# Two routing stages of a four-block graph and mixture kernel: sums, tables, semaphores and bias loads rearranged

## The reference, cut to what matters

```python
top_vals, top_idx = jax.lax.top_k(logits, K)          # K = 2, 8 or 16 experts
w = jax.nn.softmax(top_vals, axis=-1)
h = act(x @ W1[e] + b1[e])                            # gelu in the first, relu in the second
y = y + (h @ W2[e] + b2[e]) * w[..., e]               # only for the two chosen experts
```

## Time and profile before

| | us |
|---|---|
| median of 3 runs | 1710.01 (1708.18 to 1711.74) |
| the profiled execution, whole | 1711.71 |
| its span, first to last instruction | 1709.0 |
| PE busy | 1495.1 (87%) |
| DVE busy | 845.1 (49%) |
| ACT busy | 484.4 (28%) |
| POOL busy | 337.4 (20%) |

### The profile page before, as it was taken

The page is one execution under the profiler, slowest core; times in us unless marked ns, Lnnn a source line. Parts: engine busy times, 40 slices in busy tenths (PEclk is TensorE's granted clock), DMA queues, the critical chain, the costliest instruction groups (busy, mean ns, idle before and its releaser), DMA issues. The chain is left out here.

```text
span 1709.0 us, 33464 instructions
## 1 busy us (share of the span) xinstructions
PE 1495.1 (87%) x8648; PEld 1051.6 (62%) x8648; DVE 845.1 (49%) x2423; ACT 484.4 (28%) x1258; POOL 337.4 (20%) x391
## 2 busy tenths in 40 slices
PE   3796899999999999974999957897999829999976
PEld 3685654457444855544999942344666629899964
DVE  6897753333232467775222238411688652222227
ACT  2565310013000311111444433100233304445434
POOL 3000210013000300002455530000001224555530
PEclk9855899999999999985999979999999759999989
DMA  4000331124111422222223347402122245332436
GB/s 127 0 0 1 96 96 48 48 84 129 49 49 59 133 90 86 86 65 95 93 95 117 120 132 240 129 25 70 56 73 65 87 153 162 119 118 93 145 97 184
DMA packets 134635, 158.57 MB, mean 93 GB/s; under 512 B 16929, under 2 KB 119698, under 8 KB 134258
## 3 DMA queue, kind: packets, MB, share of 16 engines
q1 hardware_dynamic: 122642, 125.59, 23.4%
q0 software_dynamic: 11840, 32.12, 6.2%
q10 hardware_dynamic: 96, 0.20, 0.0%
HBM read 103.12 MB, written 57.93 MB: 94 GB/s over the span
## 5 line engine op out<-in xcount | busy, mean ns | idle before, releaser
L891 PE MATMUL layer_ps<-parts,counts 128*128 128x512 f16 x1875 | 409.1, 379 | 1.2 <-issue 0.6
L891 PEld LDWEIGHTS layer_ps<-parts,counts 128*128 (+1 forms) x1875 | 183.3, 98 | 217.7 <-issue 2.7
L1419 ACT ACTIVATE experts_hT<-experts_ps_h,experts_b_col 128x128 f32<-128x128 f32 x456 | 159.8, 367 | 102.8 <-PE experts_ps_h L1394 81.6
L1402 PE MATMUL experts_ps_y<-experts_rows,experts_hT 128*128 128x256 f32 x688 | 164.0, 381 | 1.1 <-ACT experts_hT L1419 0.2
L1357 POOL DMA_INDIRECT chosen<-experts_y,experts_row x116 | 114.6, 988 | 152.6 <-issue 130.0
L1402 PEld LDWEIGHTS experts_ps_y<-experts_rows,experts_hT 128*128 128x128 f32 x688 | 123.9, 190 | 16.7 <-ACT experts_hT L1419 3.2
L792 POOL TENSOR_TENSOR parts<-layer_rest,gru_rows 128x256 f32 (+2 forms) x75 | 54.5, 726 | 392.8 <-DVE layer_rest L767 392.8
L1346 POOL DMA_INDIRECT experts_fetched<-tokens,experts_index x120 | 116.1, 967 | 77.6 <-issue 45.1
L953 DVE COPY layer_total<-layer_ps 128x256 f32<-128x256 f32 x75 | 31.8, 425 | 183.5 <-PE layer_ps L891 180.6
L1394 PEld LDWEIGHTS experts_ps_h<-experts_xT,experts_rows 128*128 128x128 f32 x976 | 120.0, 194 | 4.0 <-DVE experts_xT L1435 0.9
L1394 PE MATMUL experts_ps_h<-experts_xT,experts_rows 128*128 128x128 f32 x976 | 120.4, 277 | 0.5 <-DVE experts_xT L1435 0.5
(11 more groups left out here) (315 smaller groups left out, 2080.1 us busy)
## 6 DMA issues: line engine op xcount, KB each, us to landing
experts_rows<-in_L_ffn_w SPq DMA_DIRECT2D x32, 512.0 KB, 5.0
gru_rows<-x SPq DMA_DIRECT2D x75, 128.0 KB, 2.1
own<-layer_own SPq DMA_DIRECT2D x75, 128.0 KB, 1.7
layer_own_in<-own SPq DMA_DIRECT2D x75, 128.0 KB, 2.1
h<-layer_out SPq DMA_DIRECT2D x50, 128.0 KB, 1.7
gru_rows<-h SPq DMA_DIRECT2D x50, 128.0 KB, 2.1
gru_rows<-chosen SPq DMA_DIRECT2D x50, 128.0 KB, 2.4
combine_y<-chosen SPq DMA_DIRECT2D x50, 128.0 KB, 2.4
```

The source lines that it names most:

```text
L891: last = nc.tensor.matmul(ps[b][:], cst.counts[:, s, bass.ds(t * P, P)], parts[:, s, :], start=s == 0, stop=s == NT - 1)
L1402: last = nc.tensor.matmul(ps_y[:, 0:D], hT[:, c, :], down[b][:, c, :], start=c == 0, stop=c == KH - 1)
L1419: nc.scalar.activation(hT[:, c, :], ps_h[c][:, 0:P], function, bias=b1_col[:, bass.ds(e * KH + c, 1)]).then_inc(hT_ready, 1)
```

## The change: what it does

1. `clear()` ahead of `route` is replaced by `hand_over()`, which only returns the list; POOL clears those semaphores inside `route`, after its constants. The barrier of L103 is gone there (it stays at the program's end).
2. DVE waits for `consts` ahead of its third instruction and no more ahead of its first.
3. `either` and `upto` are laid out [128, E, 25]. The running sum over tiles is made on DVE from `either`, ahead of the product with all ones. PE adds into one bank: (triangle minus ones) times `either`, then ones times `upto`. The product for the counts takes only the last tile's E columns. POOL makes the matrix `not_before`. The slot then takes one DVE instruction in place of three.
4. The tables of the second choice are made in two pieces, tiles 0 to 15 and 16 to 24, and PE starts on the first when it is there.
5. At the end two instructions (`second`, `free_row`) go behind the one that writes `plan.token`.
6. The output biases: for E = 16 they are loaded in `route`, behind the four experts' weights on SP. For E = 8 the load stays in `run_experts` but waits until the second gather has landed.

```diff
+    def hand_over(self):
+        old, self.held = self.held, []
+        return old
+
+    def clear_behind(self, old):
+        self.nc.clear_and_free_semaphores(old)
...
+        CUT = 2 * NT // 3
+        PIECES = ((slice(0, NT),), (slice(0, CUT), slice(CUT, NT)))
...
+                if expert_weights.b2_all is not None:
+                    sp.dma_start(expert_weights.b2_all[:], expert_weights.b2.partition_broadcast(P)).then_inc(
+                        expert_weights.b2_loaded, 16)
...
+                whole = lambda a: a[:].rearrange("p e t -> p (e t)")
+                pe.wait_ge(minus_ready, 1)
                 pe.wait_ge(picked, 1)
-                by_expert = either[:].rearrange("p t e -> p e t")
-                nc.tensor.matmul(ps_sum[:, 0:NT * E], cst.ones[:], by_expert, start=True, stop=True).then_inc(summed, 1)
-                nc.tensor.matmul(ps_rank[:, 0:NT * E], cst.before[:], by_expert, start=True, stop=True).then_inc(ranked, 1)
+                nc.tensor.matmul(ps_rank[:, 0:NT * E], not_before[:], whole(either), start=True, stop=False)
+                pe.wait_ge(running, 1)
+                nc.tensor.matmul(ps_sum[:, 0:E], cst.ones[:], upto[:, :, NT - 1], start=True, stop=True).then_inc(summed, 1)
+                nc.tensor.matmul(ps_rank[:, 0:NT * E], cst.ones[:], whole(upto), start=False, stop=True).then_inc(ranked, 1)
                 pe.wait_ge(bounds_ready, 1)
                 plan.ends_pe = tile_ends(nc, pe, plan, slice(0, E))
                 for c in range(2):
-                    pe.wait_ge(placed, c + 1)
-                    for t in range(NT):
-                        last = nc.tensor.matmul(ps_token[c][:, 0:MT], at_place[c][:, :, t], token_at[c][:, :, t],
-                                                start=t == 0, stop=t == NT - 1, skip_group_check=True)
+                    for i, piece in enumerate(PIECES[c]):
+                        pe.wait_ge(placed, c + i + 1)
+                        for t in range(piece.start, piece.stop):
+                            last = nc.tensor.matmul(ps_token[c][:, 0:MT], at_place[c][:, :, t], token_at[c][:, :, t],
+                                                    start=t == 0, stop=t == NT - 1, skip_group_check=True)
                     last.then_inc(tokens_known, 1)
...
-                dve.wait_ge(consts, 1)
...
+                    if c == 0:
+                        dve.wait_ge(consts, 1)
...
-                nc.vector.tensor_tensor(either[:], chosen[:, 0], chosen[:, 1], ALU.add).then_inc(picked, 1)
+                nc.vector.tensor_tensor(either[:].rearrange("p e t -> p t e"), chosen[:, 0], chosen[:, 1], ALU.add).then_inc(
+                    picked, 1)
+                dve.drain()
+                nc.vector.tensor_tensor_scan(upto[:].rearrange("p e t -> p (e t)"), first_of[:].rearrange("p e t -> p (e t)"),
+                                             either[:].rearrange("p e t -> p (e t)"), 0.0, ALU.mult, ALU.add).then_inc(
+                    running, 1)
...
                 dve.wait_ge(summed, 1)
-                nc.vector.tensor_tensor_scan(upto[:].rearrange("p e t -> p (e t)"), first_of[:].rearrange("p e t -> p (e t)"),
-                                             ps_sum[:, 0:NT * E], 0.0, ALU.mult, ALU.add)
...
-                nc.vector.tensor_scalar(tiles_i[:], upto[:, :, NT - 1], float(P - 1), None, ALU.add)
+
+                nc.vector.tensor_scalar(tiles_i[:], ps_sum[:, 0:E], float(P - 1), None, ALU.add)
...
-
-                nc.vector.tensor_tensor(upto[:].rearrange("p e t -> p (e t)"), upto[:].rearrange("p e t -> p (e t)"),
-                                        ps_sum[:, 0:NT * E], ALU.subtract)
-                dve.drain()
-                nc.vector.scalar_tensor_tensor(upto[:], base[:].unsqueeze(2).to_broadcast([P, E, NT]), float(P), upto[:],
+                dve.wait_ge(ranked, 1)
+                nc.vector.scalar_tensor_tensor(slot.rearrange("p t e -> p e t"), base[:].unsqueeze(2).to_broadcast([P, E, NT]),
+                                               float(P), ps_rank[:, 0:NT * E].rearrange("p (e t) -> p e t", t=NT),
                                                ALU.mult, ALU.add)
-                dve.wait_ge(ranked, 1)
-                dve.drain()
-                nc.vector.tensor_tensor(slot[:].rearrange("p t e -> p e t"),
-                                        ps_rank[:, 0:NT * E].rearrange("p (e t) -> p e t", t=NT), upto[:], ALU.add)
...
-                    nc.vector.tensor_tensor(at_place[c][:], number[:], to_all(slot_at[0][:, c], P), ALU.is_equal)
-                    if c > 0:
+                    for piece in PIECES[c]:
+                        to_all = lambda a, n: a[:, piece].unsqueeze(1).to_broadcast([P, n, piece.stop - piece.start])
+                        nc.vector.tensor_tensor(at_place[c][:, :, piece], number[:, :, piece], to_all(slot_at[0][:, c], P),
+                                                ALU.is_equal)
+                        if c > 0:
+                            dve.drain()
+                        nc.vector.tensor_tensor(token_at[c][:, :, piece], number[:, 0:MT, piece], to_all(slot_at[1][:, c], MT),
+                                                ALU.is_equal)
                         dve.drain()
-                    nc.vector.tensor_tensor(token_at[c], number[:, 0:MT, :], to_all(slot_at[1][:, c], MT), ALU.is_equal)
-                    dve.drain()
-                    nc.vector.tensor_tensor(token_at[c], token_at[c], to_all(token_code[:], MT), ALU.mult).then_inc(placed, 1)
+                        nc.vector.tensor_tensor(token_at[c][:, :, piece], token_at[c][:, :, piece], to_all(token_code[:], MT),
+                                                ALU.mult).then_inc(placed, 1)
...
+                dve.drain()
+                nc.vector.tensor_scalar(empty, code, 0.0, float(HALF), ALU.is_le, ALU.add)
+                dve.drain()
+                nc.vector.scalar_tensor_tensor(plan.token[:], code, -1.0, empty, ALU.add, ALU.add).then_inc(token_ready, 1)
                 nc.vector.tensor_scalar(second, ps_token[1][:, 0:MT], 0.0, float(NP), ALU.not_equal, ALU.mult)
-                dve.drain()
-                nc.vector.tensor_scalar(empty, code, 0.0, float(HALF), ALU.is_le, ALU.add)
                 nc.vector.tensor_scalar(free_row, code, 0.0, spare_row[:, 0:1], ALU.is_equal, ALU.mult)
                 dve.drain()
-                nc.vector.scalar_tensor_tensor(plan.token[:], code, -1.0, empty, ALU.add, ALU.add).then_inc(token_ready, 1)
...
                 nc.gpsimd.memset(first_of[:, :, 0:1], 0.0).then_inc(consts, 1)
+                nc.gpsimd.tensor_tensor(not_before[:], cst.before[:], cst.ones[:], ALU.subtract).then_inc(minus_ready, 1)
+                pool.drain()
                 iota(token_no[:], [[P, NT]], 1, -HALF)
                 iota(spare_row[:], [[0, 1]], 1, 2 * NP - HALF)
                 iota(number[:], [[1, P], [0, NT]], 0).then_inc(numbered, 1)
+                cst.semaphores.clear_behind(old)
...
-                sp.dma_start(b2_all[:], b2.partition_broadcast(P)).then_inc(b2_loaded, 16)
+                if b2_here:
+                    sp.wait_ge(fetch_done[1], 16)
+                    sp.dma_start(b2_all[:], weights.b2.partition_broadcast(P)).then_inc(b2_loaded, 16)
...
-                cst.semaphores.clear()
+                old = cst.semaphores.hand_over()
```

More of the change, by code:

```diff
@@ L1072, in tile_ends, with route @@
     return ends
-def route(nc, cst, dr, tag, E, logit, plan, expert_weights):
+def route(nc, cst, dr, tag, E, logit, plan, expert_weights, old):
     with ExitStack() as ctx:
@@ L1096, in route @@
         base = sb("base", [P, E])
-        slot = either
+        slot = either[:].rearrange("p e t -> p (e t)").rearrange("p (t e) -> p t e", e=E)
+        not_before = sb("not_before", [P, P])
         slot_f, slot_i = sb("slot_f", [P, 2, NT]), sb("slot_i", [P, 2, NT], I32)
@@ L1110, in route @@
         ps_token = [pb(f"ps_token{c}", [P, BANK]) for c in range(2)]
-        consts, numbered = sem("consts"), sem("numbered")
+        consts, numbered, minus_ready, running = sem("consts"), sem("numbered"), sem("minus_ready"), sem("running")
         gap_ready, exp_ready, picked, summed, ranked, placed, tokens_known = (
@@ L1303, in run_experts @@
         b1_col = sb("b1_col", [P, E * KH])
-        b2_all = sb("b2_all", [P, E, D])
+        b2_here, b2_loaded = weights.b2_all is None, weights.b2_loaded
+        b2_all = sb("b2_all", [P, E, D]) if b2_here else weights.b2_all
         fetched, fetch_done = weights.fetched, weights.fetch_done
```

31 lines of the change are left out of this document (15 added, 16 removed).

## The result

The kernel after takes 1702.07 us (median, 1701.25 to 1702.86), beside 1710.35 for the kernel before on the same chip: ratio 0.995, interval 0.994 to 0.996, so 8.3 us faster. It was timed beside the old one twice more, on two different chips: 1699.91 against 1709.64 (0.9942, 0.9926 to 0.9957) and 1700.97 against 1714.33 (0.9911, 0.9894 to 0.9928). The profiled execution took 1701.26 us (span 1698.8) against 1711.7 (1709.0). The forecast was 1696.4 and 13.6 us: the sign is right and most parts are, the size is too large.

The account below looks back on a forecast made before the run. PE bounds the long stages, untouched; the two routings hang on a line of small DVE instructions with PE products between. Gains of 5.8 and 7.8 us, together 13.6, give a median of 1696.4 us, range 1692.5 to 1702.

Parts of the forecast that it names:

- A: Routing entry: clearing, second barrier and the wait for constants leave DVE's path; gain 2.05 us first, 2.1 us second routing.
- B: From choices to counts: running sum ahead of the product, strided write of `either`; gain 0.1 us first, 0.2 us second.
- C: Slot computation: one DVE instruction stays where 1.83 us stood; gain 1.24 us in the first routing.
- D: Tables and products: PE starts on piece one without waiting; gain 0.87 us first, 1.6 us second including the slot.
- E: End of the routing chain: two instructions fewer before the token list is ready; gain 0.31 us in each routing.
- F: First gathers, freed of the bias loads beside them, take 2.55 us; gain 1.2 us first, 3.55 us second mixture.
- Rival 1: Table pieces run at one element per tick, so products are read later; gain 8.9 us, 1701.1; chance 0.07.
- rival 2: First gathers are slow by themselves, not by the bias, so nothing is gained there; 8.9 us, 1701.1; chance 0.11.
- Rival 3: PE's clock rises during the table products, halving the last ones' time; gain 15.6 us, 1694.4; chance 0.08.
- Rival 4: PE's clock stays at 0.50 in the expert loops; slower than before, about 1715 us; chance 0.04.
- Rival 5: Another barrier or clear takes the place of the removed one, costing 4 us; gain 9.5 us, 1700.5; chance 0.06.

Follow-up runs that it names:

- clear_back: Kernel after with the semaphores cleared and the second barrier passed ahead of route again; 1707.5 us, ratio 0.9943 to the kernel before.
- one_piece: Kernel after with the second choice's tables made whole instead of in two pieces; 1700.38 us, ratio 0.9941 to the kernel before.
- spread: Kernel after with a tile's empty slots gathering 128 different token rows in the second routing; 1700.66 us, ratio 0.9915 to the kernel before.
- best: Kernel after with spread empty rows, tables cut at column 18, first mixture's bias not held, dummy PE products; 1696.76 us, ratio 0.9897 to the kernel before.
- bias_back: Kernel after with the output biases loaded first thing in run_experts in both mixtures, as before; 1703.32 us, ratio 0.9933 to the kernel before.
- before_again: Kernel before, unchanged, run again beside itself; 1714.63 us, ratio 0.9998.
- after_3: Kernel after, unchanged, run again on another chip beside the kernel before; 1700.97 us against 1714.33.
- warm: Kernel after with unread dummy products on PE in its idle time in route; 1694.99 us, ratio 0.991 to the kernel before.

## Why the prediction was right in kind and too high in size

What each term gave, in us, against the forecast:

```
                             first routing      second routing
                            forecast  gained   forecast  gained
A  entry                      2.05     1.96      2.1      2.45
B  choices to counts          0.1      0.18      0.2      0.36
C  slot                       1.24     1.26     with D    with D
D  tables and products        0.87     0.60      1.6      1.80
E  end chain                  0.31     0.31      0.31     0.31
F  gather and what follows    1.2      0.87      3.55     2.48
sum                           5.8      5.2       7.8      7.4
```

**A** was right, and clear_back shows its larger half alone (1.3 us in each). The second routing gained 0.35 more because 0.42 us of idle without a cause, ahead of a choice instruction of the kernel before, went too; that was not in the sum:

```profile
1375.78 0.57 DVE L1165 TENSOR_REDUCE route_least<-route_key 128x25 f32<-128x400 f32 x1 [0.42 <-issue]
```

**B** took more for the strided write (0.58, forecast 0.52), less for the counts' product (0.43, 0.5). In the second routing 0.10 of its 0.36 went into a wait of the slot instruction for the rank. **C** gave what the earlier trace rows held. **E** is exact.

**D** was mis-sized: 0.60 instead of 0.87. The fit from the earlier trace rows put whole and short rows on one line, 8 steps for a row of 16 and 5 for one of 9; they cost 9.1 and 6.7. Piece two therefore came 0.22 after PE wanted it. Rival 1, one element per step, would have made 2.3 and 1.35 us and is excluded by 1.37 and 1.05. The rule quoted from the Trainium skill, "VectorE: DVE Perf Modes", section "Mode 2×_1P — pack two bf16 into one 32-bit read", would have given rival 1's time; these two pieces do not bear it out. The statement of the Trainium skill's "Vector Engine (DVE) Microarchitecture Reference", section 5.1, that alignment makes no difference, is nearer, though the pieces here lose steps that the whole rows do not. one_piece prices the cut as a whole: 0.6 us in each up to the gather.

**C and D of the second routing** were right in mechanism: PE's registers bind. By C PE's first table product came 0.85 us earlier, as forecast, and the two unbroken batches that followed gave 0.95 and not 0.74: DVE reads 6.77 us after PE's first table product, where 6.96 was expected.

**F** was the term that failed, in the second mixture: "I take 2.55 for both now". The 6.11 us were read as one cause, the load beside the gather. They were three: about 2.7 of the gather, 1.0 to 1.3 because over 120 of the 128 descriptors of each of the first two tiles (which hold 1 and 4 tokens) ask for one and the same row (2.70 in spread and 2.79 in best, against 3.64 to 3.97 in the runs without this edit and with the bias out of the way), and 1.7 to 2.2 of the bias (bias_back, and 6.11 less 3.95). So rival 2, slow by themselves, was right for a third of it, with a cause that the prediction did not have. In the first mixture the gather fell by 1.15, yet bias_back has the same 2.88 without the hold. The hold is then not shown to be the cause there. What differs is when the bias is issued: 0.80 us after the gather's start in the kernel before (4.03 to 4.22 in three executions), 1.09 in bias_back and also in best, which has 3.45. The issue comes later because the change puts two instructions between the list of tokens and the stage's end. That 0.3 us are the cause is not shown, since the same 1.09 goes with 2.88 and with 3.45; it stays open. The lateness from the held bias was there and of the size taken: step 2's products 0.20 late, 0.28 in the stretch (0.54 against bias_back).

**The sum and the time.** The terms give 12.6 of 13.6 us, and the stretches fell by more than the 10 us that were named as the test. The medians gave 8.3, 9.7 and 13.3 in three comparisons, so the larger miss of the first is not in the terms. Taken by its size alone, 8.3 us is what rivals 1 and 2 said (8.9), and 1702.07 lies outside the narrower interval given to the forecast (1693.5 to 1699.5); only the lines tell them apart. In the profiled pair the rest is 2.24 us longer with the change. Of these, 0.86 us lie between the relations' first product and the GRU's first into `gru_ps_g` (164.30 to 165.16) and 1.01 from there to the last logit (180.02 to 181.03), code that the change doesn't touch. PE's granted clock stood at its lower level (1.2 GHz) for 0.8 us longer in the one (7.3, 8.1) and 1.0 us longer in the other (26.4, 27.4). The expert loop's 16 products took 3.74 us there and 1.95 at the higher level, so about half of each of these microseconds is lost, 0.9 of the 1.9 us by this estimate.

Over fourteen executions of both kernels and their variants the first of these lengths follows the time at the lower level: 162.16 us with 5.1, 165.16 with 8.1, 166.49 with 12.9 (before_again). The second does so loosely: 179.15 with 22.1 and 181.03 with 27.4, but 178.87 with 25.3 (one_piece). The largest differences don't follow it at all: from step 5 of the second mixture to the end it took 282.5 us (after_3) to 288.8 (clear_back), with 19.5 and 21.2 us at the lower level, and 283.6 with 20.3 (after). The whole rest varies from 1631.6 to 1640.1, on both sides: before_again had 1640.07, clear_back 1639.8. So the clock is a part of it, and most of it has no cause shown here. Why the three comparisons differ by more than their intervals is open; the runs show that it is no fixed loss in the middle, and no more than that.

**The other rivals.** Rival 3, the clock rising in the table products: it stayed at 0.50, and warm shows that they would have gained nothing (3.11 us against 3.12), so its price was wrong too. Rival 4, the expert loops at the lower clock: by the third step the 16 products took 1.95 us, as before. Rival 5: L103 is gone.

The range 1692.5 to 1702.0 ends 0.07 below the first median of the kernel after and holds the other two, which stand beside other medians of the kernel before. That the first is so near the edge is owed to the rest of the program more than to the terms, which miss the sum by 1.0 us; where in the range a median falls is luck, as far as these runs show. Its low bound for F in the second mixture, 2 us, was nearly what came (2.16 from gather to copy).

## What to carry over

When a stall is longer than one cause explains, split it before booking all of it: compare the same transfer with the load beside it and without, and look at what its descriptors ask for. A chain of small instructions can be priced to a tenth of a microsecond from the trace, and here it was; what the medians show of it moves by several microseconds with the rest of the program, so judge such a change by its stretches, and end them early: to the first product each kernel repeated within 0.3 us, to the loop's third step the kernel before moved by 1.1 (42.85 to 43.95). Filling empty slots with one index is cheap in arithmetic and dear in the gather, where an expert has next to no tokens.

## What the runs showed of the hardware that was not expected

- Gathering mostly one row: 96 packets took 26.8% of the DMA engines' time in 5 us, with rows apart 17.6%; 1.0 to 1.3 us on the first gather.
- Table products of 128x64 f16, whose operands lie with a stride, took 3.11 us for 25 at a mean grant of 0.76 and 3.12 at 0.50. The f32 pairs of 200 columns went from 1.00 to 0.58 us.
- Two f16 sources in pieces of rows: 9.1, 11.0, 6.7 and 5.4 steps for 16, 20, 9 and 5 elements, where 25 in a whole row cost 13.
- A strided f32 write of 200 elements cost 0.58 us on DVE where a plain one cost 0.37.
